# Fourteen sequences start the recurrence early, the last two run alone on ScalarE, and the last layer's tiles run two ahead

## The reference

```python
h = tok(x)                                  # embedding plus a correction by domain
h = h + attention(layernorm(h))             # 16 heads, latent keys, causal
h = h + experts(layernorm(h))               # 8 experts, gated, dense
x = layernorm(h)                            # the recurrent layer, N = 64 states
conv = sum(pad(x)[:, j:j + T] * conv_w[:, j] for j in range(4))
p = (x + conv) @ in_w.T + in_b
d = tanh(x @ dt_w.T + dt_b) @ tr_w.T
state = silu(d[t] + state) + p[t]           # for t = 0 .. 127, one after the other
h = h + states @ out_w.T + out_b
x = layernorm(h)                            # the last layer, INNER = 704
h = h + fp4(silu(fp4(x) @ fp4(w_gate).T) * (fp4(x) @ fp4(w_up).T)) @ fp4(w_down).T
```

## Time and profile before

| | us |
|---|---|
| time, median of 3 runs (lowest to highest) | 600.24 (599.64 to 601.51) |
| the profiled execution's own time | 600.67 |
| span of its profile, first to last instruction | 598.7 |
| PE busy | 527.1 (88%) |
| DVE busy | 449.0 (75%) |
| ACT busy | 249.9 (42%) |
| POOL busy | 210.6 (35%) |

### The profile page before, as it was taken

One profiled execution on the slowest core, in us unless ns is written; L12 is line 12 of the kernel. 1 busy time (PEld: TensorE's weight loads), 2 busy tenths in 40 slices (PEclk: granted clock), 3 DMA queues, 4 the chain that ended last, 5 costly groups with the idle time before them and its releaser, 6 DMA issues.

```text
span 598.7 us, 9145 instructions
## 1 busy us (share of the span) xinstructions
PE 527.1 (88%) x2919; PEld 314.6 (53%) x2934; DVE 449.0 (75%) x1122; ACT 249.9 (42%) x765; POOL 210.6 (35%) x421
## 2 busy tenths in 40 slices
PE   2789999989999999999999997983669999999994
PEld 1556556456456556555555544641226565565663
DVE  1255797887888788789789777485678898988863
ACT  1273273264246236226317327413335555554330
POOL 6503253353342232223213213021336666665311
PEclk9899999999999999999999999995669999999997
DMA  6800000000000000000000000004300000000000
GB/s 184 280 2 10 9 10 12 9 9 9 9 0 9 9 0 0 0 1 0 0 0 0 0 0 2 1 1 79 61 2 9 11 18 18 10 19 10 18 19 18
DMA packets 13518, 12.76 MB, mean 21 GB/s; under 512 B 2795, under 2 KB 12724, under 8 KB 13492
## 3 DMA queue, kind: packets, MB, share of 16 engines
q1 hardware_dynamic: 12212, 10.34, 6.6%
q0 software_dynamic: 1280, 2.11, 1.3%
HBM read 8.25 MB, written 2.10 MB: 17 GB/s over the span
## 4 chain that ended last, share of the span: by engine, by line
PE 41%; DVE 17%; issue 13%; POOL 11%; ACT 10%; SPq 4%; DMA 2%; DVEq 1%; POOLq 0%; ACTq 0%
PE psum L673 13%; ACT probs L1036 6%; PE psum L948 4%; POOL rstd L449 4%; SPq L392 4%; PE psum L978 3%; PE psum L591 3%; DVE stats L1327 3%; POOL hq L509 2%; PE psum L627 2%; POOL u_now L528 2%; POOL rstd L446 2%; PE psum L739 2%; PE psum L964 2%; PE psum L613 2%
## 5 line engine op out<-in xcount | busy, mean ns | idle before, releaser
L673 PE MATMUL psum<-expw_sb,n2T 128*128 128x512 f32 x256 | 116.5, 598 | 0.0
L446 POOL TENSOR_TENSOR rstd<-meanvar,ln_eps_col 128x1 f32<-128x1 f32 x64 | 17.6, 275 | 263.5 <-DVE meanvar L1331 263.4
L948 PE MATMUL psum<-wguT,n2T 128*128 128x512 f32 (+1 forms) x192 | 82.4, 580 | 0.0
L1036 ACT ACTIVATE probs<-psum,neg_max 128x128 f32<-128x128 f32 x256 | 68.7, 405 | 5.7 <-DVE neg_max L1350 5.5
L673 PEld LDWEIGHTS psum<-expw_sb,n2T 128*128 128x128 f32 x256 | 46.2, 190 | 45.9 <-issue 45.9
L1004 ACT ACTIVATE probsT<-psum 128x512 f32<-128x512 f32 (+2 forms) x88 | 39.6, 463 | 49.2 <-PE psum L627 30.8
L948 PEld LDWEIGHTS psum<-wguT,n2T 128*128 128x128 f32 x192 | 37.9, 198 | 39.3 <-issue 34.1
L1412 DVE SCALAR_TENSOR_TENSOR acc<-psum,g_w,acc 128x256 f32<-128x256 f32 x96 | 42.0, 479 | 12.4 <-PE psum L673 8.4
L978 PE MATMUL psum<-wdT,probsT 128*128 128x256 f32 x192 | 50.4, 406 | 0.1
L1183 ACT ACTIVATE probs<-u_now 64x16 f32<-64x16 f32 x128 | 27.3, 214 | 46.9 <-POOL u_now L528 29.8
L1350 DVE TENSOR_REDUCE neg_max<-psum 128x4 f32<-128x512 f32 x64 | 40.3, 681 | 5.3 <-remote 3.0
(11 more groups left out here) (172 smaller groups left out, 973.2 us busy)
## 6 DMA issues: line engine op xcount, KB each, us to landing
expw_sb<-in_expert_w SPq DMA_DIRECT2D x8, 256.0 KB
expw_sb<-hidden SPq DMA_DIRECT2D x16, 128.0 KB
result<-res SPq DMA_DIRECT2D x16, 128.0 KB
w_raw<-in_w_down SPq DMA_DIRECT2D x1, 704.0 KB, 9.3
w_raw<-in_w_gate SPq DMA_DIRECT2D x1, 640.0 KB, 7.2
w_raw<-in_w_up SPq DMA_DIRECT2D x1, 640.0 KB, 8.1
wexp_sb<-in_w_expand SPq DMA_DIRECT2D x1, 256.0 KB, 3.1
wproj_sb<-in_w_project SPq DMA_DIRECT2D x1, 256.0 KB, 3.2
```

The lines of the kernel that those rows point to most:

```text
L673: last = mm(pq[:, g, :], n2T[:, u, k, :], expw_sb[:, k, EPQ * g:EPQ * (g + 1), :].rearrange("p e n -> p (e n)"), start=(k == 0), stop=(k = ...
L948: last = mm(pgu[u][:, c0:c1], xqT[:, u, k, :], wguT[:, k, c0:c1], start=(k == 0), stop=(k == KD - 1))
L1036: last = nc.scalar.activation(probs[:, u, h, :], pq[:, g, j * T:(j + 1) * T], ACT.Exp, bias=neg_max[:, u, h:h + 1])
```

## The change

Six things change. (1) The recurrence begins in the last pair with the 14 sequences that are ready: `width(t)` is 14 for t < 16 (`MERGE`), `gated` and `advance` work on that many columns, and gated(0) stands on ACT ahead of the last pair's last copies. (2) The last two sequences go through steps 0 to 15 alone, on ACT (`late`): one activation a step, with the step's drive as its bias, each waiting for the one before. advance(15) waits for both, and from step 16 on all 16 go together. (3) All `advance` are on POOL; DVE has none. (4) In the last pair the convolution is gone: POOL multiplies the taps into the weights (`input_weights`), and `project_in` sums eight products over shifted inputs instead of two. (5) The loop begins earlier and with less ahead: `AHEAD` is 24 and not 40, and in iteration j DVE does add_outp, x_stats, x_aggregate and all of x_fp4 of tile j + 2. x_norm from tile 2 on is on ACT. (6) Only tiles 3 and later wait for the last `turned` DMA. Four semaphores of the fp4 steps become one, and so do two of `mix`.

```diff
+        FIRST_SEQS, EARLY, MERGE = SEQS - 2, 7, 16
-        AHEAD = 40
+        AHEAD = 24
...
-                sp.dma_start(by_time[:, j, :], hidden[...]).then_inc(turned[min(j, 2)], 16)
+                sp.dma_start(by_time[:, j, :], hidden[...]).then_inc(turned[min(j, 3)], 16)
... POOL
+            def input_weights():
+                pool.wait_ge(wt_pe, WEIGHT_JOBS)
+                for k in range(KD):
+                    pool.tensor_tensor(tap_in[:, k], inw_sb[:, k, :].unsqueeze(1).to_broadcast([128, TAPS, STATE]),
+                                       convw_sb[:, k, :].unsqueeze(2).to_broadcast([128, TAPS, STATE]),
+                                       ALU.mult).then_inc(tap_weights, 1)
...
+            for t in range(EARLY, MERGE - 1):
+                advance(t)
             states(0)
             rstd_of(3, 0, 1)
             states(1)
+            for t in range(MERGE - 1, 19):
+                advance(t)
+            x_rescaled(0)
...
             for j in range(TILES):
-                for t in steps_beside(j):
+                beside = steps_beside(j)
+                for t in beside[0:6]:
                     advance(t)
-                    if t == steps_beside(j)[4] and j + 2 < TILES:
-                        x_rescaled(j + 2)
+                if j + 2 < TILES:
+                    x_shift_of(j + 2)
+                for t in beside[6:7]:
+                    advance(t)
                 (h_rescaled(j))
-                if j + 4 < TILES:
-                    pool.wait_ge(ln_aggr[3], j + 5)
-                    x_shift_of(j + 4)
-                if j + 5 < TILES:
-                    states(j + 5)
+                for t in beside[7:8]:
+                    advance(t)
+                if j + 3 < TILES:
+                    states(j + 3)
+                if j + 2 < TILES:
+                    x_rescaled(j + 2)
... PE
                     for k in range(KD):
-                        last = mm(pback[0][...], inw_sb[:, k, :], mixed[:, k, u, :], ...)
+                        for j in range(TAPS):
+                            last = mm(pback[0][...], tap_in[:, k, j, :], n3T[:, u, k, j:j + T], ...)
...
             for j in range(TILES):
-                if j + 4 < TILES:
-                    outp(j + 4)
                 if j + 1 < TILES:
                     gate_up(j + 1)
                 h_transposed(j)
-                if j + 2 < TILES:
+                if 0 < j < TILES - 2:
                     x_transposed(j + 2)
-                down(j)
+                down(j, range(4))
+                if j == 0:
+                    x_transposed(2)
+                elif j + 3 < TILES:
+                    outp(j + 3)
+                down(j, range(4, KI))
... ACT
+            def late(u, steps):
+                s = FIRST_SEQS + u
+                for t in steps:
+                    if t == 0: (as gated, of one column)
+                    else:
+                        act.wait_ge(late_done[u], t)
+                        last = nc.scalar.activation(gated_all[:, t, s:s + 1], gated_all[:, t - 1, s:s + 1], ACT.Silu,
+                                                    bias=drive[:, t - 1, s:s + 1])
+                    last.then_inc(late_done[u], 1)
...
             for j in range(TILES):
                 beside = steps_beside(j)
-                gated_beside(beside[0:5])
+                gated_beside(beside[0:4])
                 (h_sizes(j))
-                gated_beside(beside[5:6])
-                if j + 3 < TILES:
-                    x_sizes(j + 3)
-                gated_beside(beside[6:8])
-                if j + 1 < TILES:
+                gated_beside(beside[4:6])
+                if j + 2 < TILES:
+                    x_norm(j + 2)
+                gated_beside(beside[6:7])
+                if j + 2 < TILES:
+                    x_sizes(j + 2)
+                gated_beside(beside[7:8])
+                if 0 < j < TILES - 1:
                     silu(j + 1)
                 h_transposed(j)
                 if j + 2 < TILES:
                     x_transposed(j + 2)
-                if j + 4 < TILES:
-                    x_norm(j + 4)
... DVE, the loop's order after
+                for k in range(5):
+                    h_fp4(k, j)
+                if second:
+                    add_outp(j + 2)
+                    x_stats(j + 2)
+                    x_aggregate(j + 2)
+                h_fp4(6, j)
+                h_fp4(7, j)
+                if j > 0:
+                    result(j - 1)
+                if second:
+                    for k in range(5):
+                        x_fp4(k, j + 2)
+                if j == 0:
+                    h_product(1)
+                if second:
+                    x_fp4(6, j + 2)
+                    x_fp4(7, j + 2)
+                if j > 0:
+                    h_product(j + 1, FIRST if j + 2 == TILES else WHOLE)
```

More of the change, by code:

```diff
@@ L222, in tower @@
         stored = sems("stored", 2)
[L223 removed]
+        turned = sems("turned", 4)
         pool_set = sem("pool_set")
@@ L464, in convolved, with advance @@
                     pool.tensor_tensor(y, y, tap_prod[:, j, u0:u1, :], ALU.add).then_inc(conv_pool, 1)
+            def advance(t):
+                if t + 1 < T:
+                    w = width(t + 1)
+                    pool.wait_ge(silu_done, t + 1)
+                    if t + 1 == MERGE:
+                        for late in late_done:
+                            pool.wait_ge(late, MERGE)
+                    pool.tensor_tensor(u_now[:, 0:w], gated_all[:, t, 0:w], drive[:, t, 0:w],
+                                       ALU.add).then_inc(u_ready, 1)
             def body(i, front, back, rec):
@@ L488, in body @@
                     gather_behind(i, 1)
+                    if not front:
+                        input_weights()
                     rstd_of(2, 0, n[0])
                     if not front:
-                        convolved(i, 0, 0, 1)
+                        for t in range(EARLY):
+                            advance(t)
                         rstd_of(2, 1, n[1])
@@ L967, in h_transposed, with down @@
                 last.then_inc(hqT_done[1], 1)
-            def down(j):
+            def down(j, chunks):
                 u, start = j % 2, first_chunks(j)
                 wait(pe, res_ready, j)
-                for k in range(KI):
+                for k in chunks:
                     rows = min(128, INNER - 128 * k)
@@ L984, in _ @@
             x_transposed(0)
+            gate_up(0, range(2))
+            x_transposed(1)
+            gate_up(0, range(2, 3))
             outp(2)
-            gate_up(0)
-            x_transposed(1)
-            outp(3)
             for j in range(TILES):
-                if j + 4 < TILES:
-                    outp(j + 4)
                 if j + 1 < TILES:
@@ L1171, in body, with gated @@
                 if last_pair:
+                    for t in range(2, 6):
+                        gated(t)
                     rank_inputs(0, 1, 0)
+                    for t in range(6, EARLY + 1):
+                        gated(t)
                     recurrence_transposed(1)
+                    late(0, range(2))
+                    gated(EARLY + 1)
+                    late(0, range(2, 4))
                     rank_inputs(1, 2, 0)
-            over_pairs(act, body)
-            def gated(t):
-                if t == 0:
-                    act.wait_ge(d_stored, SEQS)
-                wait(act, u_ready, t)
-                nc.scalar.activation(gated_all[:, t, :], u_now[:], ACT.Silu).then_inc(silu_done, 1)
+            def gated(t):
+                w = width(t)
+                if t == 0:
+                    act.wait_ge(d_stored, FIRST_SEQS)
+                else:
+                    act.wait_ge(u_ready, t)
+                nc.scalar.activation(gated_all[:, t, 0:w], u_now[:, 0:w], ACT.Silu).then_inc(silu_done, 1)
+            def late(u, steps):
+                s = FIRST_SEQS + u
+                for t in steps:
+                    if t == 0:
+                        act.wait_ge(d_stored, s + 1)
+                        last = nc.scalar.activation(gated_all[:, t, s:s + 1], u_now[:, s:s + 1], ACT.Silu)
+                    else:
+                        act.wait_ge(late_done[u], t)
+                        last = nc.scalar.activation(gated_all[:, t, s:s + 1], gated_all[:, t - 1, s:s + 1], ACT.Silu,
+                                                    bias=drive[:, t - 1, s:s + 1])
+                    last.then_inc(late_done[u], 1)
+            over_pairs(act, body)
             def x_transposed(j):
@@ L1652, in _ @@
                 x_fp4(k, 0)
-                advance(15 + k)
             add_outp(1)
-            advance(20)
             x_fp4(6, 0)
+            x_fp4(7, 0)
             x_stats(1)
-            advance(21)
-            x_fp4(7, 0)
             x_aggregate(1)
-            advance(22)
-            advance(23)
             x_norm(1)
-            for k in range(5):
+            for k in range(8):
```

(28 more changed lines are left out.)

160 lines of the change are left out of this document (77 added, 83 removed).

## The result

The changed kernel takes 628.63 us (median of 4 runs, 624.99 to 629.78) where the kernel before, run beside it, takes 600.66 (599.64 to 601.51): ratio 1.045, 95% interval 1.041 to 1.049. Slower, as forecast, but 10 us more than the 618.6 and just outside the range (595 to 627).

A forecast was written before the change was run, and what follows sets the result against it. In the loop TensorE (9.39 us an iteration at most) and DVE were nearly full; in the filling stage TensorE mostly waited. 26.1 lost in 13 iterations minus 7.8 gained is +18.3, giving 618.6 us, range 595 to 627.

The forecast's parts named there:

- Trade of a shorter filling stage for a longer loop: Whole change: filling stage shortened once, tile's x closer to its use in 13 iterations; break-even at an iteration of 9.99.
- Filling stage, 7.8 gained: Before the loop: h_fp4(0) of tile 1 starts at 443.0 instead of 450.76; gain between 3.3 and 9.6 us.
- Late steps 0.31, early start worth 0.3: Last two sequences on ACT: 0.31 us per late step; states(0) at 415.35 instead of 415.69, buying 0.3.
- Iteration of 11.4 by the locks: Loop: POOL and DVE keep each other out, delaying x_norm and x_fp4; an iteration takes 11.4 us instead of 9.39.
- the case forecast at 11.2: Loop: if POOL gets one more small operation between h_fp4(6) and (7), an iteration takes 11.2 instead of 11.65.
- the rival that they are harmless: Loop: POOL's small operations get through beside h_fp4(6), (7); x_fp4(7) ends at 9.95 to 10.3; 600 to 605 us; chance 0.20.
- 13 x 2.01 = 26.1 lost: Loop: 13 iterations at 11.4 instead of 9.39 lose 26.1 us.
- would idle 2 us in each of these iterations: Loop: TensorE, with 9.39 of work at most, idles 2 us in each longer iteration.
- the rival of 0.11: More than forecast: four extra table loads, 622 to 624 us, or TensorE's clock falling, 640 and up; chance 0.11.
- Stretch after tile 14 unchanged: After h_fp4(0, 14): same work in the same order, so its 25.9 us to the span's end stays.
- The semaphores at nothing: Fp4 steps and `mix`: the semaphores made one were costed at nothing.
- the ring of 9.7: Loop: a tile's x hangs on the previous tile's x by a closed ring, 9.7 us with engines otherwise free.

The follow-up runs named there:

- experiment 6: Kernel before with split `turned` waits, shared semaphores, last pair's tap weights and the early start; filling order and loop as before: 599.00 us, ratio 0.9938.
- experiment 5: Kernel before with split `turned` waits, shared semaphores, and tap weights with projection over shifted copies replacing the last pair's convolution: 599.28 us, ratio 0.9946.
- Experiment 1: Changed kernel with h_fp4(6) and (7) of tiles 0 to 14 taking their second operand from PSUM, output differing: 608.93 us, ratio 1.0085.
- experiment 8: Changed kernel with x_norm from tile 2 on DVE, POOL's shift dropped, x_fp4(0..4) ahead of h_fp4(6) and (7): 641.6 us, ratio 1.0643.
- experiment 9: Changed kernel with x_norm from tile 2 on DVE behind result(j-1), POOL's shift dropped, h_fp4(6) and (7) left first: 636.37 us, ratio 1.0594.
- experiment 12: Experiment 11 with three more unread matmuls on TensorE ahead of the x tile's transposes: 627.44 us, ratio 1.0439.
- experiment 2: Changed kernel with three unread matmuls filling TensorE's gap ahead of x_transposed in the loop: 623.25 us, ratio 1.0348.
- experiment 4: Kernel before with only the `turned` waits split by tile and the fp4 steps on shared semaphores: 600.98 us, ratio 0.9958.
- experiment 11: Experiment 10 with add_outp to aggregate behind h_fp4(3), result(j-1) before h_fp4(6), h_sizes behind three gated steps, x_shift_of behind three advances: 636.64 us, ratio 1.0583.
- experiment 10: Changed kernel with outp(j+3) ahead of down, add_outp to aggregate behind h_fp4(0), x_shift_of behind two advances, x_norm behind h_sizes: 641.69 us, ratio 1.0682.
- experiment 7: Experiment 4 with eight unread matmuls in TensorE's waits of the filling stage: 603.22 us, ratio 1.0006.

## Why the prediction was right, and where it failed

- **Trade of a shorter filling stage for a longer loop**: right, and shown by experiment 6.
- **Filling stage, 7.8 gained**: 8.2. The total was right, a part of it by luck. `drive` was forecast at 409.6 and came at 411.6 net of the offset: the second sequence's sixteen matmuls took 3.39, at a granted clock of 0.56, where the first's took 1.97 at 1.00. ACT had to wait 1.59 for it, a wait that the forecast didn't have. That states(0), forecast at 415.35, still came at 415.3 is because the 18 late and six gated steps took 5.6 and not 6.8: where the two late sequences take turns, four steps go in 0.85 and not in 1.24. Behind states(0) the steps fit: h_fp4(0, 0) at 432.1 for 432.4, iteration 0 10.5 for 10.6.
- **Late steps 0.31, early start worth 0.3**: seven in a row in 2.25 are 0.32 each, right. The early start's 0.3 is neither shown nor refuted: experiments 5 and 6 differ by 0.3 us, which their intervals don't tell from zero, and in their profiles states(0) is 0.2 later with it. The gain at states(0), 0.4 us in the changed kernel, is there without it: experiment 5 has it 0.5 earlier than before.
- **Iteration of 11.4 by the locks**: 11.32 at full clock. The advance beside h_fp4(6), x_shift_of beside h_fp4(7), x_norm 1.3 late and x_fp4(1) behind hq are all in the trace. The first of x_shift_of, 0.18, got in between h_fp4(6) and (7) (510.80), which is the case forecast at 11.2. Experiment 1 shows that the locks are 1.10 of it; the rival that they are harmless is refuted. Its 9.95 to 10.3 for a ring without their cost is where experiment 1 came, 10.22. The Trainium skill's rule, in SBUF — State Buffer, "Who interferes with whom", agrees in both directions for VectorE operations with two SBUF inputs: GpSimd was held by them (0.81 and 0.83), and one was held by GpSimd (1.49 in experiment 8). The 1.57 and 1.42 of experiments 9 and 12 are TENSOR_SCALAR operations with one such input, for which that section says only that they can contend.
- **13 x 2.01 = 26.1 lost**: 25.1 at full clock. Here the forecast stopped.
- **The failed step**: that TensorE "would idle 2 us in each of these iterations" was written down with no price, so the sum has nothing for what follows the wait. The idle time was right, 2.08. Behind such waits TensorE's clock falls, in every second iteration from the fifth on and in the first two: 9.7 us beyond 13 x 11.32, of which experiment 2 shows 7.2 to be the clock's. I had it as a part of the rival of 0.11, priced at 13 or more for every iteration and argued against from a 2 us window of a pair with 0.66 idle. That row could not carry it: it shows no single wait of 2 us. Experiments 2 and 12 show the clock as a loss of its own. With 9.7 in the sum the forecast would have been 628.3.
- **The range**: by its own terms the forecast reached 628, and 627 was given.
- **Table loads**: one at the first Silu, 1.28; none at the two Tanh that follow a Silu. That half of the rival is refuted. The Trainium skill's 2.66 for a switch of tables stands in ScalarE: Activation LUTs, "What ACT_TABLE_LOAD costs", and not in the section that the prediction names. The trace is shorter: 1.31 from the end of the operation before the load (398.55) to the start of the one behind it (399.86).
- **Stretch after tile 14 unchanged**: +0.6, no more than other profiles with the same code there differ (24.96 in experiment 4, 25.85 before).
- **The semaphores at nothing**: no run has them alone. With the split waits for `turned` (part 6) they are worth 0.4% in the kernel before.
- **Open**: what closes the remaining 0.83 (10.22 against 9.39) without locks. I read it as the ring of 9.7 with its waits. Experiments 8 to 11 each tried to take the 1.34 wait away and got other waits or longer operations for it, so none proves it.

The best versions are experiments 5 and 6, 0.5 to 0.6% under before, and 5% under the changed kernel.

## What to carry to other kernels

When a change makes TensorE wait longer in each iteration, price the slower matmuls behind the wait too, and don't argue them away from a row that has no such wait in it. Take a gain of the filling stage only after the loop's ring is counted with every in-order queue that it runs through (here POOL's advance, ACT's gated step, Silu): four tries to remove a 1.34 us wait made the iteration longer and not shorter (at full clock 11.60, 11.74 and 12.5 to 12.6 instead of 11.32, in experiments 11, 9 and 10; in experiment 8 the clock never came up). Before an operation is moved to VectorE, see which long GpSimd operation it will begin beside.

## What was not expected of the hardware

- The clock can alternate: 1.00 in one iteration of 11.32 and 0.86 in the next of 12.50, from the fifth iteration on, with a wait of 2.08 ahead of the fall and one of 1.57 ahead of the matmuls at 1.00. Once, at 482.23, the eight matmuls took 1.89 behind 2.09 too. In experiment 1, with waits of 0.98 in iterations of 10.22, it stayed at 1.00; in experiment 7 down took 3.79 behind a wait of 2.75, and 3.04 behind 1.06 in experiment 4.
- Silu and Tanh worked after one table load.
- A 128 x 16 VectorE operation took 1.42 instead of 0.17 beside a GpSimd operation of 1.38 that began 0.01 after it in the profile: its size did not protect it.
- Two ScalarE steps of 64 x 1 that wait for each other take 0.32 each (seven in 2.25); where two such chains take turns, four steps took 0.85.
